# Attention scores of 8 tokens per matmul, in four groups of 32 TensorE columns, in a fused attention and expert kernel

## The reference, cut to what matters

```python
q = (x @ Wq + bq).reshape(b, s, h, d)          # h = 4 heads, d = 256; k and v alike
qr, qi = (q * c, q * sn);  kr, ki = (k * c, k * sn)
scores = (einsum('bshd,bsgd->bshg', qr, kr) + einsum('bshd,bsgd->bshg', qi, ki)) / 16
attn = softmax(scores, axis=-1)                # over the 4 heads g of the same token s
out = einsum('bshg,bsgd->bshd', attn, v)
...
x = x + attention(xn) * silu(xn + experts(xn))
```

## Time and profile before

| | |
|---|---|
| median of 3 runs | 1698.37 us (1698.24 to 1698.8) |
| the profiled execution's own time | 1698.34 us |
| its span from first to last instruction | 1696.6 us |
| busy: TensorE matmul / VectorE / ScalarE / GpSimd | 97% / 58% / 43% / 46% of the span |

### The profile page before, as it was taken

One profiled execution on the slowest core, in us unless ns is written; L12 is line 12 of the kernel. 1 busy time (PEld: TensorE's weight loads), 2 busy tenths in 40 slices (PEclk: granted clock), 3 DMA queues, 4 the chain that ended last, 5 costly groups with the idle time before them and its releaser, 6 DMA issues.

```text
span 1696.6 us, 28609 instructions
## 1 busy us (share of the span) xinstructions
PE 1643.0 (97%) x9360; PEld 1276.8 (75%) x9360; DVE 988.6 (58%) x1879; ACT 733.4 (43%) x1205; POOL 785.1 (46%) x945
## 2 busy tenths in 40 slices
PE   5998999989999999999999999999999999999998
PEld 3556676578888888888888888776877668776785
DVE  7568988843333333333333335768777786777766
ACT  5773432513333333333333335355454564535542
POOL 4647577614333433343433442534544646345362
PEclk9999999999999999999999999999999999999998
DMA  9988733162313131313111412424556345552354
GB/s 331 398 319 311 265 107 125 63 263 89 128 51 128 56 124 57 125 57 125 54 54 57 156 54 84 162 101 160 180 180 199 124 155 178 189 182 97 126 168 137
DMA packets 162662, 250.96 MB, mean 148 GB/s; under 512 B 13928, under 2 KB 121248, under 8 KB 161376
## 3 DMA queue, kind: packets, MB, share of 16 engines
q1 hardware_dynamic: 147904, 211.47, 35.8%
q0 software_dynamic: 12960, 35.41, 6.3%
q10 hardware_dynamic: 1664, 2.26, 0.4%
HBM read 149.58 MB, written 99.50 MB: 147 GB/s over the span
## 4 chain that ended last, share of the span: by engine, by line
PE 88%; DVE 6%; DMA 4%; ACT 1%; issue 1%; POOL 0%; ACTq 0%; SPq 0%; DVEq 0%
PE ps L1140 21%; PE ps L1075 19%; PE ps L1022 13%; PE ps L1086 12%; PE ps L1159 10%; PE ps L1149 3%; DMA AUX<-xn_d,AUX 3%; PE ps L1043 2%; PE ps L1122 2%; PE ps L993 2%; PE ps L921 1%; PE ps L911 1%; PE ps L977 1%; DVE WM L1590 1%; DMA WR<-w_d 1%
## 5 line engine op out<-in xcount | busy, mean ns | idle before, releaser
L1140 PE MATMUL ps<-WR,FR 128*128 x1620 | 414.6, 406 | 5.1 <-issue 3.3
L1140 PEld LDWEIGHTS ps<-WR,FR 128*128 128x128 f32 x1620 | 300.7, 192 | 65.6 <-issue 6.7
L646 POOL DMA_INDIRECT y_d<-AUX x135 | 133.7, 990 | 371.6 <-ACT AUX L865 371.6
L1650 DVE TENSOR_TENSOR AUX<-AUX,ps 128x512 f32<-128x512 f32 x135 | 92.9, 688 | 352.7 <-ACT AUX L853 352.7
L814 ACT ACTIVATE WM<-ps,bcs,trig 128x512 f32<-128x512 f32 x256 | 255.7, 1018 | 88.2 <-PE ps L1075 80.5
L1590 DVE TENSOR_SCALAR WM<-ps,vec,trig 128x512 f32<-128x512 f32 x256 | 246.2, 995 | 62.4 <-ACT WM L814 61.8
L1022 PE MATMUL ps<-WM 128*128 128x128 f32 x2048 | 236.3, 277 | 7.2 <-DVE TM L1478 7.2
L1022 PEld LDWEIGHTS ps<-WM 128*128 128x128 f32 x2048 | 232.0, 193 | 14.7 <-DVE TM L1478 8.0
L1086 PE MATMUL ps<-WM,XTJ 128*128 128x512 f32 x512 | 237.1, 600 | 0.0
L853 ACT ACTIVATE AUX<-ps 128x512 f32<-128x512 f32 x135 | 80.9, 599 | 329.0 <-PE ps L1140 329.0
L1159 PE MATMUL ps<-WR,ABR 128*128 x1080 | 209.5, 292 | 0.0
(11 more groups left out here) (237 smaller groups left out, 2282.5 us busy)
## 6 DMA issues: line engine op xcount, KB each, us to landing
US<-u_d SPq DMA_DIRECT2D x63, 512.0 KB, 4.7
u_d<-UN SPq DMA_DIRECT2D x120, 256.0 KB, 2.0
WR<-w_d SPq DMA_DIRECT2D x8, 3072.0 KB
AUX<-y_d SPq DMA_DIRECT2D x32, 512.0 KB, 5.7
WM<-in_L_attn_x_dram SPq DMA_DIRECT2D x16, 512.0 KB, 9.6
xn_d<-WM SPq DMA_DIRECT2D x32, 256.0 KB, 6.8
w_d<-USR SPq DMA_DIRECT2D x16, 512.0 KB, 5.1
AUX<-xn_d SPq DMA_DIRECT2D x16, 512.0 KB, 6.5
```

Of the source, the lines that this page charges most:

```text
L646: e.indirect_dma_start(y_d, bass.IndirectOffsetOnAxis(toks[:, m - 5:m - 4], 0), YS[:, (m - 5) % 2, :], None).then_inc(s_y[(m - 5) % 2], 16)
L1140: mm = e.matmul(b[:, :], x, WR[:, bass.ds(off[m] + (2048 * z + 1024 * a + 512 * k), 512)], start=(k == 0 and x is xh and z == 0), stop=(k ...
L1650: e.tensor_tensor(HS[:, m % 2, :], GR[:, :], mP[m % 2][:, :], ALU.mult).then_inc(s_h, 1)
```

## The change

The scores of a group are computed for 8 tokens at a time instead of 32. The stationary operand is now 32 columns (8 tokens x 4 heads), the moving operand 32 columns (4 heads x 8 tokens). Four such matmuls, `a` = 0 to 3, take the place of one; they write the four partition groups of the same bank (rows 0 to 31, 32 to 63, ...), and `a` is the innermost loop. The result of a group is 128x128 instead of 128x512, the mask is `mask8`, and `soft_a`'s first two operations read a quarter of the elements. The sums, their order of accumulation and everything after them stay.

```diff
                 for c in range(4):
-                    col = 128 * (4 * (n % 4) + c)
                     for x in range(2):
                         for h in range(2):
-                            mm = e.matmul(pS[n % 2][:, 128 * c:128 * c + 128].rearrange("p (g t) -> p g t", g=H),
-                                          QT[:, x, h, col:col + 128],
-                                          QT[:, 2 + x, h, :].rearrange("p (g t) -> p g t", g=H)[:, :, col // 4:col // 4 + 32],
-                                          start=(x == h == 0), stop=(x == h == 1))
+                            for a in range(4):
+                                row = 32 * a
+                                col = 128 * (4 * (n % 4) + c) + row
+                                mm = e.matmul(pS[n % 2][row:row + 32, 32 * c:32 * c + 32].rearrange("p (g t) -> p g t", g=H),
+                                              QT[:, x, h, col:col + 32],
+                                              QT[:, 2 + x, h, :].rearrange("p (g t) -> p g t", g=H)[:, :, col // 4:col // 4 + 8],
+                                              start=(x == h == 0), stop=(x == h == 1))
                 mm.then_inc(s_s, 1)
...
-            diag = maskt[:, None, :].broadcast_to([128, 4 * H, 32])
+            diag = mask8[:, None, :].broadcast_to([128, 4 * H, 8])
...
-                e.tensor_tensor(TM[:, :].rearrange("p (x t) -> p x t", t=32),
-                                pS[n % 2][:, :].rearrange("p (x t) -> p x t", t=32), diag,
+                e.tensor_tensor(TM[:, 0:128].rearrange("p (x t) -> p x t", t=8),
+                                pS[n % 2][:, 0:128].rearrange("p (x t) -> p x t", t=8), diag,
                                 ALU.mult).then_inc(s_sm1, 1)
...
-                ch(e.tensor_reduce(SS[:, n % 2, :], TM[:, :].rearrange("p (x t) -> p x t", t=32), AX.X, ALU.add))
+                ch(e.tensor_reduce(SS[:, n % 2, :], TM[:, 0:128].rearrange("p (x t) -> p x t", t=8), AX.X, ALU.add))
```

## The result

The kernel after the change takes 1756.54 us (median of 4, 1754.75 to 1764.16) against 1698.59 us of the kernel before in the same session: ratio 1.034, 95% interval 1.031 to 1.037. It is **slower by 3.4%**, where I forecast 1599 us. The profiled execution has a span of 1753.9 us, 57.3 us more than before.

What follows compares the result with a forecast made beforehand. TensorE was taken to bound the kernel, with the scores as work on the critical path. Savings of 77, 3.4, 10, 3 and 6 us, 99.4 together, brought the 1696.6 us span to 1597.2, plus 1.74 around it 1599 us; range 1565 to 1650.

Steps and rivals of the forecast that it cites:

- the bound on the fetch: Scores on TensorE: one fetch packet a group, at least 2.0 us if asked for only when the last is used up; upper bound 2.4.
- 1.8 us a group: TensorE's scores: a group of 128 pairs at 14 ns each, between 0.9 and 2.4 us, instead of 3.58 us.
- the 77 us to be saved in batches 4 to 14: Scores stages: 7.3 us instead of 14.32 us, 7.0 saved, times 11 batches.
- The signs that I had written for being wrong: Scores weight loads over 20 ns apart, microsecond gaps ending with fetch packets, clock under 1 behind stages, chunk matmuls waiting for VectorE.
- Slower: instructions come too slowly: Rival, 10%: TensorE's scores stream slower than 28 ns a pair; at line 1053's 60 ns, +246 us, 1944; at 35 ns, +54 us.
- The clock rival: Rival, 10%: small matmuls may count as little work, so the clock falls; 1.75 us lost after each of 16 stages, 1627 us.
- 14 ns a pair: Issue rate of matmul and weight load pairs in the scores, taken as twice the burst's 7 ns because the stream is long.
- The burst of eight in `mix`: Eight weight loads of `mix` starting 7 ns apart, after work that let the queue fill; 0.9 us for 128.
- 0.29 us for both operations: VectorE's lines 1478 and 1482: 0.69 us each becomes about 0.29, and between 0.29 and 0.38; no wait on TensorE.
- batches 1 and 2 gain less because of VectorE and GpSimd: VectorE also makes one-hot tiles there, busy 40.9 of 44 us, GpSimd 40.5; 5 us saved each, 10 in all.
- Batch 3 and the end: Batch 3: groups three and four fall from 7.41 to 3.6 us, 3 us saved; batch 15 at the end: 6 us saved.
- The silu that I feared would be late: ScalarE's silu after chunk 18, batches 5 to 15, waits 1.1 us for GpSimd's sum; hidden from TensorE, otherwise 4 us in all.

Runs made afterwards that it cites:

- VectorE's part alone: The kernel before with only the change to the mask, the product and the sum, leaving most scores out of the sums: 1695.99 us, ratio 0.9995.

## Why the prediction was wrong

The step that failed is the bound on the fetch: "If each packet were asked for only when the last is used up, a group would last at least as long as a short DMA takes to land, 2.0 us; with some issue on top I put the upper bound at 2.4." The sum's term that rests on it, 1.8 us a group, came out as 4.1 us (16.40 / 4), and the 77 us to be saved in batches 4 to 14 as 43.2 us lost. The mechanism was named, and the count (one packet a group) was right, but the price was taken from the wrong row. A round of the fetch is 3.5 to 4.0 us with nearly idle DMA engines (the run with later loads) and 3.5 to 7.6 us, 5.5 on average, in the traffic of the scores stage. I had the landing of one small DMA and left out the time behind it (1.2 to 1.6 us to the first matmul), and I did not ask what the queues hold in that stage, although SyncE issues its loads of values and expert results just there. The stage hides none of it: three rounds are needed in a batch (four in batch 10), since the first burst is 107 to 235 matmuls of 512 in batches 4 to 15. The signs that I had written for being wrong, gaps of a microsecond with a fetch packet at the end and a clock under 1 behind the stages, are the ones that came.

The rival that came true is "Slower: instructions come too slowly", to which I gave 10%. Its point of decision was 28 ns a pair; a stage of 512 pairs in 16.40 us is 32 ns. The price per batch (2.1 us) follows from it; its 60 ns did not occur. (The row behind that figure gives 0.40 us for four matmuls, up to the end of the last; 0.24 us is up to the start of the next one. They are bf16, too, unlike the scores.)

The clock rival came true as well, as a consequence and not for the reason I gave: 1.8 us a batch, where I had written 1.75. With the same matmuls between the chunks, and next to no stands, the clock stays full.

The issue rate was better than I took: 14 ns a pair forecast; 128 matmuls whose own length is 0.197 us take 1.28 us from the first start to the last end (the burst at 1154.34), so 127 steps take 1.08 us, 8.5 ns each. The burst of eight in `mix`, with 7 ns, was the nearer row, as long as the instructions are there. The Trainium skill's 60 cycles a matmul (TensorEngine Tiling (Array Packing), Instruction Overhead), an estimated 25 ns at full clock, do not hold for the matmuls here, which go round four column groups: the measured 8.5 ns decides.

VectorE: 0.29 us for both operations, as said (0.29, and 0.29 to 0.38); that this part is hidden was right (VectorE's part alone: nothing). That batches 1 and 2 gain less because of VectorE and GpSimd was not tested, since the stands cover it. Batch 3 and the end did not gain for the same reason. The silu that I feared would be late is no wait of TensorE in any run.

What turned the gain into a loss was one thing: the scores' own work fell by 131 us, and 151.5 us of standing on the fetch took its place; most of the rest of the loss is the 30.6 us that TensorE's other matmuls took longer.

## What to carry to other kernels

Count instructions as well as columns. Once what is in hand is used up, a stream of short matmuls here was bound by the fetch, because 256 instructions took 1.3 us and a packet's whole round 3.5 to 7.6 us in the traffic of that stage; the sign was bursts of exactly one packet's instructions with "issue" between them. At 3.7 us for 256 instructions (64 columns, a stage of two packets) the stands were all but gone. So either halve the instructions (two groups of 64 columns, 5.2% faster than before), or put long matmuls between short ones (4.6%; 6.4% with both), and look at the clock only after the stands are gone.

## What the runs showed of the hardware that I had not expected

- TensorE's instructions come in packets of 16 KB (256 instructions of 64 bytes). With 256 instructions used in 1.3 us the next packet is not there: a round is 3.5 to 4.0 us at a DMA share of 0.07 to 0.10 in the stage, and 3.5 to 7.6 us in stages with a share of 0.61 to 0.84.
- Four column groups taken in turn issue float32 pairs of 32 columns every 8.5 ns; two column groups of 64 take 29 ns a pair (1.87 us for 64), near the 28 ns that half of the 56 ns by columns would give.
- TensorE's granted clock fell to the lower level in stages in which it was busy 6 us of 14 to 19, and stayed there for 4 and 5.4 us of dense chunks behind the two shown. It did not fall in the batches where the same matmuls stood between chunks, next to without a stand.
- Going from 128-column to 64-column matmuls and back costs about 0.1 us a group even with nothing to wait for (2.02 against 1.9 us), and the moved order as a whole about 1 us a batch.
